# Attention with conditioning on one core: the score and maxima matmuls contract over 128 rows instead of 98 and 96

## The reference, cut to what matters

```python
x = x.reshape(8, 512, 512)                   # float32
Q = split_heads(x @ Wq.T + bq)               # 16 heads of 32
K = split_heads(x @ Wk.T + bk)
V = split_heads(x @ Wv.T + bv)
cQ = Q + split_heads(cond @ Wq.T + bq)       # cond: one row of 512 for each batch
cK = K + split_heads(cond @ Wk.T + bk)
attn = softmax(cQ @ cK.T / sqrt(32))         # over the keys, 512 x 512 for each head
out = x + merge_heads(attn @ V)
```

## Time and profile before

| | |
|---|---|
| median of 3 runs | 655.18 us (654.62 to 655.79) |
| profiled execution, first to last instruction (its span) | 654.2 us |
| TensorE matmul busy | 647.3 us, 99% of the span |
| VectorE / ScalarE / GpSimd busy | 540.6 / 389.6 / 487.4 us |

### The profile page before, as it was taken

The page is one execution under the profiler, slowest core; times in us unless marked ns, Lnnn a source line. Parts: engine busy times, 40 slices in busy tenths (PEclk is TensorE's granted clock), DMA queues, the critical chain, the costliest instruction groups (busy, mean ns, idle before and its releaser), DMA issues.

```text
span 654.2 us, 10054 instructions
## 1 busy us (share of the span) xinstructions
PE 647.3 (99%) x3528; PEld 442.8 (68%) x3528; DVE 540.6 (83%) x815; ACT 389.6 (60%) x684; POOL 487.4 (74%) x204
## 2 busy tenths in 40 slices
PE   9999999999999999999999999999999999999997
PEld 6776677666677666676666776666776666776542
DVE  5776888888888888888888888888888888888787
ACT  6455666565566565666556665556665555564773
POOL 6338877778877779777779777779777788666992
PEclk9999999999999999999999999999999999999999
DMA  8944333555333555333554434553434544424501
GB/s 260 255 97 115 103 107 87 143 147 140 97 110 94 144 147 132 97 108 103 146 146 125 104 96 114 146 147 107 116 90 127 146 131 124 119 67 110 151 18 65
DMA packets 48038, 79.87 MB, mean 122 GB/s; under 512 B 9458, under 2 KB 9714, under 8 KB 47986
## 3 DMA queue, kind: packets, MB, share of 16 engines
q1 hardware_dynamic: 47632, 79.07, 45.1%
q10 hardware_dynamic: 356, 0.16, 0.1%
HBM read 19.95 MB, written 8.39 MB: 43 GB/s over the span
## 4 chain that ended last, share of the span: by engine, by line
PE 95%; DVE 2%; issue 1%; ACT 1%; DMA 1%; ACTq 0%; POOLq 0%; DVEq 0%
PE bank L350 27%; PE bank L442 18%; PE bank L420 18%; PE bank L462 16%; PE bank L398 14%; DVE bank L737 1%; PE bank L368 1%; ACT Pt L637 1%; DMA Qs<-mt 1%; DVE part_sums L762 0%; DVE rr L786 0%; DVE ends L807 0%; PE bank L470 0%; DVE rr L775 0%; DVE bank L793 0%
## 5 line engine op out<-in xcount | busy, mean ns | idle before, releaser
L637 ACT ACTIVATE Pt<-bank 128x512 f32<-128x512 f32 x512 | 299.2, 600 | 216.3 <-PE bank L442 144.8
L737 DVE TENSOR_REDUCE mf<-bank 128x1 f32<-128x512 f32 x496 | 332.6, 686 | 72.3 <-PE bank L420 69.3
L943 POOL TENSOR_TENSOR A<-A,Pt 128x2048 f32<-128x2048 f32 x59 | 270.9, 4592 | 4.6
L442 PE MATMUL bank<-Qs,Ks 98*128 98x512 f32 x496 | 197.5, 404 | 1.4 <-DMA Qs<-mt 1.4
L420 PE MATMUL bank<-Ks,Qs 96*128 96x512 f32 x496 | 197.6, 399 | 0.2
L943 POOL TENSOR_TENSOR A<-Pt 128x2048 f32<-128x2048 f32 x30 | 138.4, 4614 | 9.3 <-DVE part_sums L762 9.3
L442 PEld LDWEIGHTS bank<-Qs,Ks 98*128 98x128 f32 x496 | 93.1, 188 | 52.1 <-ACT Pt L637 25.9
L462 PE MATMUL bank<-Pt,V 128*32 128x512 f32 x1024 | 118.9, 596 | 0.0
L913 POOL TENSOR_TENSOR Xl<-xr,Xh 128x512 fp32r<-128x512 f32 x28 | 36.1, 1291 | 110.0 <-ACT Xh L598 110.0
L420 PEld LDWEIGHTS bank<-Ks,Qs 96*128 96x128 f32 x496 | 93.8, 189 | 26.7 <-DVE bank L737 3.0
L350 PE MATMUL bank<-Xh,Wl 128*128 128x512 f32 x256 | 102.2, 399 | 0.0
(11 more groups left out here) (73 smaller groups left out, 389.4 us busy)
## 6 DMA issues: line engine op xcount, KB each, us to landing
Qs<-hi SPq DMA_DIRECT2D x60, 256.0 KB, 3.6
Ks<-hi SPq DMA_DIRECT2D x60, 256.0 KB, 3.6
Qs<-lo SPq DMA_DIRECT2D x30, 256.0 KB, 4.1
Ks<-lo SPq DMA_DIRECT2D x30, 256.0 KB, 3.4
xr<-xT SPq DMA_DIRECT2D x28, 256.0 KB, 2.7
res<-xT SPq DMA_DIRECT2D x28, 256.0 KB, 2.9
outT<-ot SPq DMA_DIRECT2D x28, 256.0 KB, 3.1
Qs<-mt SPq DMA_DIRECT2D x122, 4.0 KB
```

What stands on the lines that cost most here:

```text
L442: e.matmul(st_bank(u)[:, :], k[0:98, j, kc * P:(kc + 1) * P], q[0:98, j, :], start=True, stop=True).then_inc(t_st, 1)
L637: e.activation(exponentials(g)[:, kc, j, :], st_bank(u)[:, :], ACT.Exp, scale=SCALE).then_inc(a_e, 1)
L737: e.reduce_max(to[:, 4 * j + qc:4 * j + qc + 1], MXB[u % 2][:, :], AXX).then_inc(v_mx, 1)
L943: e.tensor_tensor(sums, ex[:, 0, :, :] if kc == 1 else sums, ex[:, kc, :, :], ALU.add).then_inc(p_a, 1)
```

## The change

Both matmuls contract over all 128 rows of the two tiles. Rows 98 to 127 of `Qs` are zero, written once; rows 96 to 127 of `Ks` are -1. Since maxima now read rows 96 and 97 too, these two must be zero in `Qs` until the group's maxima are done and the maxima rows are written there: for each new group in a used slot (28 of them: 3 to 31 without 28) a DMA copies rows 98 and 99, which are zero, over rows 96 and 97. It is issued between the wait for `t_st` and the wait for `a_hi`, and counts toward `stack_landed`, which waits for 4 DMAs instead of 3 for Q from a slot's second use on. The waits for `p_ks` and `d_ks` move from the first scores to the first maxima of a group, and `v_z` is new there. In group 28 the one DMA of two rows into `Xl` becomes 32 rows, and two more, of 30 and 2 rows, fill `Xh`.

```diff
         def stack_landed(e, qk, g):
             home, n = stack_home(g)
-            e.wait_ge(d_st[home][qk], 16 * 3 * n)
+            e.wait_ge(d_st[home][qk], 16 * (3 * n + (n - 1 if qk == 0 else 0)))
...
                 if m == 0:
                     stack_landed(e, 0, g)
                     stack_landed(e, 1, g)
-                e.matmul(MXB[u % 2][:, :], q[0:96, j, qc * P:(qc + 1) * P], k[0:96, j, :],
+                    if g < NSLOT:
+                        e.wait_ge(p_ks, g + 1)
+                        e.wait_ge(v_z, g + 1)
+                    if g == G - 4:
+                        e.wait_ge(d_ks, 48)
+                e.matmul(MXB[u % 2][:, :], q[:, j, qc * P:(qc + 1) * P], k[:, j, :],
...
                 if n == 0:
                     e.wait_ge(d_mr[g % 2], 64 * (g // 2 + 1))
-                    if g < NSLOT:
-                        e.wait_ge(p_ks, g + 1)
-                    if g == G - 4:
-                        e.wait_ge(d_ks, 16)
...
-                e.matmul(st_bank(u)[:, :], k[0:98, j, kc * P:(kc + 1) * P], q[0:98, j, :],
+                e.matmul(st_bank(u)[:, :], k[:, j, kc * P:(kc + 1) * P], q[:, j, :],
...
+            def no_maxima(sl):
+                e.memset(Qs[96:128, sl, :, :].bitcast(F32), 0.0).then_inc(v_z, 1)
...
             e.memset(ones[:, :], 1.0).then_inc(v_c, 1)
+            no_maxima(0)
...
             qk_lo(1, 0)
-            for qk in (0, 1):
-                qk_lo(qk, 1)
+            no_maxima(1)
+            qk_lo(0, 1)
+            no_maxima(2)
+            qk_lo(1, 1)
...
-                e.memset(Ks[96:98, sl, :, :].bitcast(F32), -1.0).then_inc(p_ks, 1)
+                e.memset(Ks[96:128, sl, :, :].bitcast(F32), -1.0).then_inc(p_ks, 1)
...
                 if g >= NSLOT and g != G - 4 and qk == 0:
                     e.wait_ge(t_st, SLOTS * (stack_before(g) + 1))
+                if g >= NSLOT and g != G - 4 and qk == 0:
+                    e.dma_start(dst[96:98, :, :].bitcast(F32),
+                                dst[98:100, :, :].bitcast(F32)).then_inc(d_st[sl][qk], 16)
                 e.wait_ge(a_hi, 2 * g + qk + 1)
...
-                    e.dma_start(Xl[96:98, 0, :, :].bitcast(F32), Ks[96:98, 0, :, :].bitcast(F32)).then_inc(d_ks, 16)
+                    e.dma_start(Xl[96:128, 0, :, :].bitcast(F32), Ks[96:128, 0, :, :].bitcast(F32)).then_inc(d_ks, 16)
+                    e.dma_start(Xh[98:128, 0, :, :].bitcast(F32), Qs[98:128, 0, :, :].bitcast(F32)).then_inc(d_ks, 16)
+                    e.dma_start(Xh[96:98, 0, :, :].bitcast(F32), Qs[98:100, 0, :, :].bitcast(F32)).then_inc(d_ks, 16)
```

More of the change, by code:

```diff
@@ L172, in cond_attention @@
         v_c = sem("v_c")
+        v_z = sem("v_z")
         v_b2 = sem("v_b2")
```

## The result

The changed kernel takes **644.26 us** (median of 4 runs, 644.02 to 645.23), against 655.43 us for the kernel before timed beside it: ratio 0.9823, 95% interval 0.98 to 0.9846. By the medians that is 11.2 us less. The forecast was 642.0 us, 13.2 us less. The profiled execution took 645.23 us by its own time, its span is 643.4 us, and the span of before was 654.2: 10.8 us less.

What follows compares the result with a forecast made beforehand. TensorE's summed steps were taken to bound the kernel (93% of the chain). 15.0 - 1.2 - 0.6 = 13.2 us less brings the span from 654.2 to 641.0, plus 1.0 gives 642.0 us; 8-in-10 range 639.5 to 655.6.

Steps and rivals of the forecast that it cites:

- The step: TensorE's 512-column matmuls: with one row count, 0.2340 us falls to 0.2265; about 2000 steps, 15.0 us gained.
- the argument from the opening: Opening projections, all full-row, take 0.2265 us a step; steps lengthen from the first 96-row maxima matmul at 20.20 us.
- The doubt named in it, tiles and banks: Scores and maxima also read stacked tiles and change bank at each matmul, perhaps causing slow steps; called the largest doubt.
- The side work at no cost: Memsets on VectorE and GpSimd, 28 two-row copies, group 28's extra rows and moved waits: all hidden, cost 0.
- The late groups: Four groups, 531 to 610 us, with VectorE 87% busy: 1.8 us of gain, less 0.6 us for hold-ups.
- The slots of three: Three-matmul slots shrink to 0.680 us, 6 ns below VectorE's reduction; the 0.03 us lag is absorbed by two banks.
- VectorE as the releaser of maxima in each group: Sign in the profile after that the claim of hidden memsets and copies was wrong; no size given.
- The recovery after the values burst, 0.04 us, 31 times: Steps behind each burst of value matmuls with 32 output columns must settle again: 1.2 us off the gain.
- From span to median: Whole kernel: the median lies 1.0 us above the profiled span, so a span of 641.0 gives 642.0 us.
- Nothing: Rival for scores and maxima: they disturb as such, rows play no part; time stays about 655 us; chance 0.13.
- Half: Rival: partial rows are one cause, bank or tile changes at scores and maxima another; 648.6 us; chance 0.12.
- slower: Rival: full-row operands cost scores and maxima matmuls 3 ns more each, 3.1 us in all; 658.3 us; chance 0.13.

Runs made afterwards that it cites:

- e8: Changed kernel with two projection matmuls of group 1, one of Q's and one of K's chain, contracting over 96 rows: 644.2 us in one run.
- e5: Changed kernel with scores, maxima and all projections contracting over 96 rows: 646.19 us against 654.66 for the kernel before, ratio 0.9868.
- e3: Changed kernel with scores back at 98 rows and maxima at 96, keeping memsets, copies and moved waits: 654.63 us against 654.66 for the kernel before, ratio 0.9999.
- spread kernel: Changed kernel with projections of groups 1 to 24 redistributed so each group's last slots have four matmuls, not three: 642.78 us, ratio 0.9822 to the kernel before.
- e6: Changed kernel with VectorE's row maxima taken over 448 of 512 columns: 643.02 us against 654.61 for the kernel before.

## Why the prediction was right, and where its size was off

*The step.* Right. 0.2340 us became 0.2270, and the durations 389 ns; the argument from the opening held as it stood. e8 shows the cause apart from tiles, banks and waits. Only its wording was off: not "a matmul of 96 or 98 rows disturbs", but a row count other than the neighbour's does, as 96 rows everywhere settle as well (e5). And in e8 it is three full-row matmuls behind the odd one that are longer, and the fourth is at 389, where the prediction had about four.

*The doubt named in it, tiles and banks.* Unfounded: e8, and e3 beside e5.

*The side work at no cost.* Right, 0.03 us by e3. VectorE's memset is 1.76 us, at the lower bound of 1.8 and not the 2.2 taken; GpSimd's does not grow with rows; the copies' issues are over before K's wait ends.

*The late groups.* The forecast had 1.8 less 0.6, 1.2 us. Groups 25 to 28 took 610.16 - 529.93 = 80.23 us before and take 599.20 - 520.12 = 79.08 now: 1.15 us. The first row of each fence is the start of group 1.

```profile
55.76 0.40 PE L442 MATMUL bank<-Qs,Ks 98*128 98x512 f32 x1
...
529.93 0.39 PE L442 MATMUL bank<-Qs,Ks 98*128 98x512 f32 x1
...
610.16 0.47 PE L442 MATMUL bank<-Qs,Ks 98*128 98x512 f32 x1
```

```profile
54.75 0.39 PE L445 MATMUL bank<-Qs,Ks 128*128 128x512 f32 x1
...
520.12 0.40 PE L445 MATMUL bank<-Qs,Ks 128*128 128x512 f32 x1
...
599.20 0.47 PE L445 MATMUL bank<-Qs,Ks 128*128 128x512 f32 x1
```

*The slots of three.* "With some five such slots in a group VectorE falls 0.03 us behind, which two banks absorb." This is the term that was mis-sized. It stood at nothing, and measures 0.09 us a group. VectorE's lag in these slots was not measured against what it started with: it comes to them with a low part's subtraction just done (304.25 us), and six reductions follow without a pause, each 0.68 to 0.69 us long where a slot is 0.68. TensorE catches it up in every group. One of the prediction's own signs of being wrong in the side work came with it, "VectorE as the releaser of maxima in each group", though by e3 it is not the side work that makes it (1.6 us, 8 times in its list, as before). The waits of maxima for VectorE went from 1.6 to 6.5 us in the list, 8 to 32 times, most of it overlapped by the matmul in flight; at 305.70 us the loss is 0.05 us, and the steps behind it must settle again, which costs as much once more (2.35 against 2.27 us for the ten steps there; 0.09 on the mean of groups 3 to 23 in this trace). In the spread kernel these ten steps take 2.27 us. Groups 1 to 24 take 463.9 us there, so the table gives back (465.37 - 463.9) / 24 = 0.06 us a group. It is not the full 0.09, as the steps behind the burst cost 0.03 us more on the mean in that kernel; why, no run shows. By e6 and its trace, what is left without the stop is VectorE's as well, and not late exponentials.

*The recovery after the values burst, 0.04 us, 31 times.* Right: the ten steps from 312.35 to 314.67 us take 2.32 where settled ones take 2.27, and 0.04 us more on the mean of groups 3 to 23. A settled step is 0.2267 us (45 of them from 314.67 us on take 10.20), 7.3 ns under 0.2340. So a group gains 66 x 7.3 ns = 0.48 us by the step, less 0.04 for the recovery and 0.09 for VectorE: 0.35, where 0.35 to 0.37 is measured. Nothing of size is left over.

*From span to median.* The 1.0 us held (0.9), but by luck: an execution is 1.8 us longer than its own span (645.23 and 643.4), and the profiled one happened to be the slowest of its four. The difference of 13.2 us does not rest on it.

*The rivals.* "Nothing" is refuted by e3 beside the kernel after: only the rows differ, and the gain goes with them. The Trainium skill, page "TensorE: Matmul & The Clock Gate", section "Step-by-step: what each phase is for", says of loading weights that the row count "doesn't matter here". So far as e5 has the same step with 96 rows as with 128, the traces agree. The cost lies between matmuls of different counts, of which that sentence does not speak: 7 ns on about 2000 steps are 14 us, of which 11 are left after the recovery, the late groups and VectorE. "Half" is out by e8 and e3, "slower" by the durations.

## What to carry to other kernels

Where TensorE sets the time, give neighbouring matmuls the same number of contraction rows, if need be by zero rows: a difference of one row was nearly as dear as of 30 and 32 here, 3% of each step. All of this was seen with one shape alone, loads of 128 columns and matmuls of 512. Look for it in the durations: 389 ns where one shape stands alone, 393 to 401 where shapes are mixed. And when the bound engine becomes 3% faster, compare its shortest slot with the next engine's work for it; the one that was 0.702 us before was 0.680 afterwards, against reductions of 0.69, and some 2 of a possible 13 us went there, of which spreading the work brought back 1.3. A lateness of 0.03 us that no list of waits shows is enough to unsettle the steps behind it.

## What was not expected of the hardware

One matmul of another row count lengthens itself and the next three by 6, 10, 6 and 4 ns (e8). In the kernel before the three full ones at 544.5 to 545.0 us, behind two partial ones, are longer by 6, 6 and 4 ns, and the fourth is at 389, in projections of the other kind. 127 rows beside 128 cost nearly what 96 do. And the state doesn't depend on how many rows there are: 96 everywhere and 128 everywhere both give 389 ns.
